# Message pass of a graph network: the gathered rows are added by VectorE instead of by TensorE

## The reference, cut to what matters

```python
em = jnp.concatenate([x[src], x[dst]], axis=-1)
em = jax.nn.relu(layer_norm(em @ msg_w + msg_b, msg_g, msg_beta))
em = em * edge_weights[:, None]
msgs = jax.ops.segment_sum(em, dst, num_segments=num_nodes)
```

## Time and profile before

| | |
|---|---|
| median of three runs | 8413.61 us |
| the profiled execution, its own time | 8343.49 us |
| its span | 8341.7 us |
| PE, PEld, DVE busy | 70%, 62%, 56% of the span |
| POOL, ACT busy | 55%, 36% |
| granted PE clock, whole span | 0.735 |
| two attention passes and what surrounds them | 0 to about 5743 us |
| message pass | about 5743 to 8224 us |
| update of the nodes | the rest |

### The profile page before, as it was taken

How to read it: one execution, slowest core, us unless ns; L and a number is a source line. 1 busy time by engine, 2 the same in 40 slices (tenths; PEclk the granted TensorE clock), 3 DMA queues, 4 the chain that set the end, 5 groups by cost and what they waited for, 6 DMA issues and landing times. The chain is left out here.

```text
span 8341.7 us, 141114 instructions
## 1 busy us (share of the span) xinstructions
PE 5805.1 (70%) x33726; PEld 5162.1 (62%) x33726; DVE 4669.5 (56%) x15714; ACT 2995.0 (36%) x10333; POOL 4625.8 (55%) x4876
## 2 busy tenths in 40 slices
PE   4666777767767727788888788866666666666665
PEld 3555566656656626777777777756666656666664
DVE  4555555555555654545554455455555555556557
ACT  2333333333333322222222222235555555555556
POOL 4555555555555326666666666623666666666661
PEclk6777777777777756656666656668888888888887
DMA  7333333333333232222222222231111111111111
GB/s 161 108 83 85 84 84 84 87 86 84 84 85 85 58 101 51 53 52 51 51 53 51 51 51 52 53 86 41 44 44 44 45 44 44 45 44 44 44 44 29
DMA packets 334794, 535.96 MB, mean 64 GB/s; under 512 B 105502, under 2 KB 222767, under 8 KB 333665
## 3 DMA queue, kind: packets, MB, share of 16 engines
q0 software_dynamic: 181264, 439.20, 20.8%
q1 hardware_dynamic: 143462, 83.65, 3.8%
q10 hardware_dynamic: 9323, 4.08, 0.2%
HBM read 489.59 MB, written 42.61 MB: 64 GB/s over the span
## 5 line engine op out<-in xcount | busy, mean ns | idle before, releaser
L976 POOL DMA_INDIRECT arena<-rows,slot_src x3222 | 3078.8, 956 | 2167.7 <-issue 856.0
L759 POOL DMA_INDIRECT arena<-msg_rows,slot_src x1611 | 1521.9, 945 | 963.2 <-remote 543.7
L1173 ACT ACTIVATE arena<-psum 128x512 f32<-128x512 bf16 x808 | 480.6, 595 | 2291.4 <-remote 1609.0
L1077 PE MATMUL psum<-arena 128*128 x3232 | 738.0, 371 | 707.4 <-DVE arena L1255 518.5
L2141 PE MATMUL psum<-arena 128*128 128x129 f32 x3232 | 564.6, 326 | 826.1 <-DVE arena L1443 690.5
L1248 DVE TENSOR_TENSOR arena<-arena,psum 128x512 f32<-128x512 f32 x808 | 554.7, 687 | 1021.1 <-remote 658.2
L1062 PE MATMUL psum<-arena 128*128 128x145 f32 x3232 | 1082.8, 430 | 0.0
L1077 PEld LDWEIGHTS psum<-arena 128*128 128x128 f32 x3232 | 582.2, 244 | 801.5 <-issue 789.2
L2141 PEld LDWEIGHTS psum<-arena 128*128 128x128 f32 x3232 | 473.5, 224 | 908.8 <-issue 769.6
L1443 DVE TENSOR_TENSOR arena<-arena,psum 128x129 f32 x1616 | 468.4, 290 | 956.8 <-remote 667.6
L1077 PE MATMUL psum<-a_src_a_dst,arena 128*128 x3232 | 685.2, 333 | 434.1 <-DVE arena L1291 403.0
(11 more groups left out here) (361 smaller groups left out, 9910.6 us busy)
## 6 DMA issues: line engine op xcount, KB each, us to landing
arena<-rows,slot_src POOLq DMA_INDIRECT x3222
arena<-msg_rows,slot_src POOLq DMA_INDIRECT x1611
arena<-slot_keys SPq DMA_DIRECT2D x100, 128.0 KB
edge_alpha<-arena SPq DMA_DIRECT2D x50, 128.0 KB
arena<-edge_alpha SPq DMA_DIRECT2D x50, 128.0 KB
slot_keys<-lane_keys SPq DMA_DIRECT2D x24, 256.0 KB
arena<-rows SPq DMA_DIRECT2D x6, 1024.0 KB, 10.2
rows<-arena SPq DMA_DIRECT2D x4, 822.0 KB
```

Of the source, the lines that this page charges most:

```text
L759: pool.indirect_dma_start(out=self.buffer[:, v % U, j, :], out_offset=None, in_=self.source, in_offset=bass.IndirectOffsetOnAxis(ap=K.SRC[ ...
L976: pool.indirect_dma_start(out=E.rowbuf[:, r, j, :], out_offset=None, in_=E.source, in_offset=bass.IndirectOffsetOnAxis(ap=K.SRC[:, at:at + ...
L1077: return pe.matmul(E.psX[:, j, 0:E.dcol], E.onehotT[:, v % 2, j, :], rows_.rearrange("p b w -> p (b w)"), start=True, stop=True)
L1173: act.activation(E.onehotT[:, v % 2, :, :], E.psT, ACT.Copy).then_inc(E.turned, 1)
```

## The change

PE leaves the addition to DVE. The matmuls with the identity go; the picked rows alone are in PSUM, and one DVE instruction adds the four gathered tiles to them and writes the sum to the SBUF buffer `rhs`, which the later steps read. A new event `selected` goes from PE to DVE; `summed` is now signalled by DVE. Its waiters are what they were: POOL before a gather, ACT before the copy at line 801 and before the squares; PE now waits for it too, before it picks rows into a bank again.

```diff
@@ message_pass
-    summed, squared, rooted, inverted, scaled, ready, scattered = (
+    selected, summed, squared, rooted, inverted, scaled, ready, scattered = (
...
-        scaled.wait(pe, i, v - U)
-        gather.arrived.wait(pe, i, v)
+        summed.wait(pe, i, v - U)
         for j in range(G):
-            pe.matmul(psH[b][:, j, :], onehotT[:, b, j, :],
-                      K.by_dst[:, bass.ds(blocks(v, j), 1), :].rearrange("p b w -> p (b w)"), start=True, stop=False)
-            last = pe.matmul(psH[b][:, j, :], K.ident[:, :], rowbuf[:, b, j, :], start=False, stop=True)
-        last.then_inc(summed.at(v), 1)
+            last = pe.matmul(psH[b][:, j, :], onehotT[:, b, j, :],
+                             K.by_dst[:, bass.ds(blocks(v, j), 1), :].rearrange("p b w -> p (b w)"), start=True, stop=True)
+        last.then_inc(selected.at(v), 1)
+        selected.wait(dve, i, v)
+        gather.arrived.wait(dve, i, v)
+        scattered.wait(dve, i, v - U)
+        dve.tensor_tensor(rhs[:, b, :, 0:F], psH[b], rowbuf[:, b, :, :], ALU.add).then_inc(summed.at(v), 1)
         summed.wait(act, i, v)
         scaled.wait(act, i, v - U)
         for j in range(G):
-            last = act.activation(junk[:, b, j, :], psH[b][:, j, :], ACT.Square, accum_out=squares[:, b, j:j + 1])
+            last = act.activation(junk[:, b, j, :], rhs[:, b, j, 0:F], ACT.Square, accum_out=squares[:, b, j:j + 1])
...
-        scattered.wait(dve, i, v - U)
         inverted.wait(dve, i, v)
         for j in range(G):
-            last = dve.scalar_tensor_tensor(rhs[:, b, j, 0:F], psH[b][:, j, :], rstd[:, b, j:j + 1],
+            last = dve.scalar_tensor_tensor(rhs[:, b, j, 0:F], rhs[:, b, j, 0:F], rstd[:, b, j:j + 1],
                                             K.vec["L1_gnn_msg_g"], ALU.mult, ALU.mult)
```

More of the change, by code:

```diff
@@ L2043, in message_pass @@
     psH = [K.ps[:, 4 + b, :].rearrange("p (g e) -> p g e", g=G) for b in range(U)]
-    summed, squared, rooted, inverted, scaled, ready, scattered = (
-        Event(K, "message_" + x) for x in ("summed", "squared", "rooted", "inverted", "scaled", "ready", "scattered"))
+    selected, summed, squared, rooted, inverted, scaled, ready, scattered = (
+        Event(K, "message_" + x) for x in ("selected", "summed", "squared", "rooted", "inverted", "scaled", "ready", "scattered"))
     gather = Gather(K, "message", K.prow, rowbuf, [summed])
```

## The result

| | before | after |
|---|---|---|
| median, same chip | 8376.0 us (7 runs) | 8439.1 us (7 runs) |
| ratio | | 1.0077, 95% interval 1.0054 to 1.0100 |
| profiled execution | 8343.5 us | 8404.1 us |
| first and last gather issue of the message pass | 5743.4, 8192.7 | 5722.4, 8246.2 |
| a visit of that pass | 6.08 us | 6.26 us |

The change makes the kernel slower, as forecast, but by 63 us and not by 318. The message pass grew by 74.5 us (2523.8 against 2449.3). In this one execution it began 21 us earlier and the part behind its last gather took 7 us more; together these give the 60.6 us between the two profiled executions.

The account below looks back on a forecast made before the run. Bound: a loop of waits in the message pass, with PE's signals reaching others late, in bundles, while POOL issues (the held signal). 0.74 + 0.05 = 0.79 us a visit, times 403, adds 318 us to 8413.6: forecast 8730 us, range 7960 to 8850.

Parts of the forecast that it names:

- The matmuls with the identity, gain 0: PE, message pass: removing them saves 1.83 us a visit beside the wait for PE's signals, so 0 on the path.
- The waits that moved, 0: Message pass: PE's wait for rows moves to DVE, its wait for `scaled` becomes one for `summed`; old events, cost 0.
- the square and the scaling, hidden: Reading SBUF: ACT's squares 295 against 278 ns, hidden in idle time; DVE's scalings 347 against 346 ns, cost 0.
- The addition, +0.74 us a visit: DVE, message pass: POOL waits for `selected`, then DVE's 0.69 us addition, each visit; +0.74 us, between 0 and 0.97.
- The contention, +0.05 (0 to 0.25): Message pass: scalings with both inputs in SBUF slow POOL's issues; 0.05 us a visit, at most 0.25.
- The sum: Message pass: 0.74 + 0.05 = 0.79 us a visit, times 403, is 318 us.
- The held signal goes away (0.30): Rival, message pass: POOL no longer waits for PE, late bundles of PE's signals dissolve; 5.0 us a visit, 7982 us; chance 0.30.
- The addition hides in the bundle (0.15): Rival, message pass: shorter PE work brings `selected` a bundle earlier; round stays 6.07 us, 8414 us; chance 0.15.
- A round that loses two waits (0.05): Rival, message pass: DVE's longer chain makes the scatter miss its bundle one round in five; 8890 us; chance 0.05.
- The stages ahead of the pass: Stages ahead of 5743 us: should not move; if they do, the argument from one loop falls.
- the likeliest case alone: The forecast without its rivals, chance 0.50: 8640 us (0.6 us a visit) to 8850 (0.97 plus some contention).

Follow-up runs that it names:

- e2: Kernel after, with four matmuls with the identity put back ahead of the picks, their product overwritten, so PE's turn is as long as before: 1.0099, 8301.7 us.
- e1: Kernel before, with PE's matmuls with the identity left out and nothing in their place: 1.0057, 8259.3 us against 8211.5.
- e7: Kernel before, with a one-column memset on DVE between PE's sums and POOL, whose signal frees POOL: 1.0006, 1.0004, 0.9998 and 1.0004.
- e6: Kernel before, with POOL waiting once for two visits and PE still adding the rows: 1.0000, 1.0000, 0.9995 and 0.9998.
- e3: Kernel after, with a second, unused DVE addition of the same shape ahead of the one that frees POOL: 1.0244 to the kernel before.
- e5: Kernel after, with PE's picks reading blocks 0 to 3 at fixed addresses instead of addresses from a register: 1.0107 to the kernel before.
- f3: Kernel after, with DVE's addition cut in two so that its first quarter frees POOL: 0.9998 to the kernel before, 8216.2 us.
- d1 to d3: Three kernels run beside each other: e6, the cut addition of f3, and e7, each a third time: 0.9995, 1.0004 and 0.9998 to the kernel before.

## Why the prediction was right and wrong

- **The matmuls with the identity, gain 0**: right in this kernel, where the picks end 3.8 us or more ahead of the additions that wait. e2 puts as many back and loses nothing that can be told (1.0099 against 1.0077, intervals overlapping). e1 takes them away alone and wins nothing (1.0057), but changes the bursts, so it is no clean test. The size was read too high: 1.83 us a visit counts records that overlap; PE's turn gets 0.9 us shorter at the higher clock.
- **The waits that moved, 0; the square and the scaling, hidden**: right; 297 and 348 ns as priced, ACT idle for 864.9 us before its squares as before.
- **The addition, +0.74 us a visit: the step that failed.** Its mechanism was right: `selected` comes with the bundle, DVE adds in 0.69 us, POOL starts 0.96 us behind the bundle, which is 0.73 more than before. The count was wrong. I wrote that the events of the loop are the same, so one wait a visit; in the kernel after it is one wait for two visits. The pause behind eight grows from 2.11 to 2.78 us, which is 0.34 us a visit, and one pause fewer in two visits gives 0.18 back: +0.16 in place of +0.74. What makes the bursts of eight is open. It is not PE's shorter turn in this kernel (e2), though that alone can make some (96 of e1's 301 pauses, with POOL freed by PE and at its old distance from the bundle). Being freed by DVE or the later start remain; e7, the kernel that would part them, met no held signals in four runs, nor did e6, which would price a pair with PE adding, in four.
- **The contention, +0.05 (0 to 0.25)**: right in kind and size, 0.04.
- **The sum**: 0.16 + 0.04 = 0.20 us a visit for 0.79, 81 us for 318. Measured are 74.5 us in the pass and 63 us in the medians. This sum was made after the result; its parts come from the same traces.
- **The held signal goes away (0.30)**: didn't happen. Its argument was that POOL no longer waits for PE. In the kernel after POOL doesn't, and the bundles stay; in e6 on the other chips POOL does, and there are none. Both rows speak against that link. The time it gave, 5.0 us a visit, is that of any of these kernels where signals aren't held.
- **The addition hides in the bundle (0.15)**: half true, and the nearest in time (8414 us). The second visit's addition is hidden, the first's is not; and the reason given, PE's shorter turn, isn't what does it, since e2 has a full turn and the same bursts. A case between this rival and the forecast, one addition hidden in two, was missing from my list.
- **A round that loses two waits (0.05)**: no; the scatter at 7116.34 and the one behind it are served.
- **The stages ahead of the pass** took 5722 us against 5743, within what single executions differ by.

The direction was right. That the time lies in the range is no merit of the sum: the range reached down to 7960 us for a rival that didn't come, and the likeliest case alone began at 8640 us.

## What to carry to other kernels

A stall put into a loop costs its length times how often the loop waits, and the change itself can alter that count. Before multiplying by the visits, look in the trace for the rounds that cover more than one (here the first rounds, with pauses behind 8 and 20 issues, which price them). Where an instruction in such a loop frees several buffers at once, cut it so that the first buffer is freed first: here the pause was 2.33 us in place of 2.78, and no loss could be told. And compare a second chip before you tune against a wait that the trace can't name.

## What the runs showed of the hardware that was not expected

- Held signals belong to where the program runs. The kernel before takes 8376, 8212 and 8211 us where they occur and 6704 to 6725 us where they don't, a fifth less; nothing in the kernels e1, e2, e3, e5 and f3 removed them. Whether it is the chip, the core or the moment isn't known: two groups reported as the same chip, 17 minutes apart, differ (d1 to d3 without, f3 with). What the mechanism is stays open; a register address in the picks (e5) and POOL's waiting for PE (the kernel after) are excluded.
- The pause is not fixed: it grows with the burst, from 1.39 us of pause behind four issues to 2.11 behind eight and 3.67 behind twenty, and the kernel after has 4.93 behind 24, the addition included.
- PE's clock took more than half of PE's saving. With a third of its fp32 matmuls of each visit gone, PE's busy time in the pass fell by 12%, from 1618 to 1426 us, while the granted clock went from 0.85 to 0.71. A visit kept PE busy for 3.65 us where it was 4.02, 0.37 less, while the shorter turn alone is worth 0.86 at the higher level: the turn with the picks fell from 2.54 to 1.71 us, and the scatter rose from 1.39 to 1.79. It cost nothing in the kernel after, because others waited for signals and not for matmuls; in e1 slow picks did end 73 of POOL's pauses.
